# First attention of a two-layer kernel: where the turned row maxima are written, and when

## The reference

```python
qkv = x @ w_in.T + b_in                      # x: 16 batches, turned to 512 positions x 128 channels
q, k, v = jnp.split(qkv, 3, axis=-1)         # 8 heads of 16 channels each
scores = jnp.einsum('bqhd,bkhd->bhqk', q, k) / jnp.sqrt(jnp.asarray(d, q.dtype))
band = jnp.abs(idx[:, None] - idx[None, :]) <= local_size          # 64
scores = jnp.where(band[None, None], scores, neg)
attn = jax.nn.softmax(scores, axis=-1)
o = jnp.einsum('bhqk,bkhd->bqhd', attn, v).reshape(n, t, e)
o = o @ w_out.T + b_out
o = jnp.transpose(o, (0, 2, 1))
y = jax.nn.relu(o) * encodings
out = jnp.einsum('nit,io->not', y, w_ct) + b_ct[None, :, None]
```

## Time and profile before

| | |
|---|---|
| median of the runs | 1466.54 us |
| span of the profiled execution (the page gives no other time of it) | 1463.7 us |
| busy over the span | PE 1354.5 us (93%), DVE 1002.8 us (69%), ACT 791.5 us (54%), POOL 249.2 us (17%) |
| first attention | about the first 490 us of the span |
| its stationary stretch, 130 to 434 us | PE 289.27 us, DVE 290.92 us, ACT 251.25 us of 304 us, full TensorE clock |
| maxima turned (L511) | 32 times, 36.2 to 459.9 us |

### The profile page before, as it was taken

One profiled execution on the slowest core, in us unless ns is written; L12 is line 12 of the kernel. 1 busy time (PEld: TensorE's weight loads), 2 busy tenths in 40 slices (PEclk: granted clock), 3 DMA queues, 4 the chain that ended last, 5 costly groups with the idle time before them and its releaser, 6 DMA issues. The chain is left out here.

```text
span 1463.7 us, 28639 instructions
## 1 busy us (share of the span) xinstructions
PE 1354.5 (93%) x8666; PEld 813.1 (56%) x8666; DVE 1002.8 (69%) x3234; ACT 791.5 (54%) x1802; POOL 249.2 (17%) x265
## 2 busy tenths in 40 slices
PE   3678999999999799999989999999789999999998
PEld 1345555555555444444455555555434777777774
DVE  8889999999997646456546788887659654545211
ACT  4777888888888733332357677776530233332331
POOL 4100000000000100000010000002411255555552
PEclk7699999999999999999999999999999999999999
DMA  8534344343440300000020000000322588888885
GB/s 261 145 87 99 91 107 106 86 119 90 107 104 17 145 1 0 0 0 0 0 75 15 16 16 14 14 1 2 146 85 93 184 247 251 255 257 246 255 233 115
DMA packets 63186, 149.52 MB, mean 102 GB/s; under 512 B 10792, under 2 KB 27830, under 8 KB 58892
## 3 DMA queue, kind: packets, MB, share of 16 engines
q1 hardware_dynamic: 49836, 115.70, 26.1%
q0 software_dynamic: 13280, 32.93, 9.6%
HBM read 113.21 MB, written 35.39 MB: 102 GB/s over the span
## 5 line engine op out<-in xcount | busy, mean ns | idle before, releaser
L776 DVE CUSTOM_DVE_ANT_0 masked_scores<-ps_max,band_mask 128x192 bf16<-128x192 f32 (+1 forms) x512 | 177.2, 383 | 20.5 <-PE ps_max L505 13.9
L383 ACT ACTIVATE probs_t<-ps_sc 128x448 f32<-128x448 f32 x256 | 138.7, 542 | 80.4 <-PE ps_sc L525 78.1
L1255 PE MATMUL f_ps<-f_xt,w_t 128*128 (+1 forms) x704 | 160.2, 382 | 2.5 <-ACT w_t L1310 2.5
L377 ACT ACTIVATE nf_above<-nf_scaled,nf_sign_at 128x512 f16<-128x512 bf16 x231 | 161.5, 715 | 0.0
L2803 DVE TENSOR_TENSOR d_inter<-d_silu_g,d_su 128x384 f32<-128x384 f32 x32 | 17.7, 554 | 159.6 <-PE d_su L2487 154.4
L1927 ACT ACTIVATE c_probs<-d_sg,c_negmax 128x128 f32<-128x128 f32 x256 | 90.3, 365 | 58.1 <-DVE c_negmax L2012 57.7
L1255 PEld LDWEIGHTS f_ps<-f_xt,w_t 128*128 128x128 bf16 x704 | 69.3, 98 | 86.7 <-issue 5.0
L2320 POOL DMA_INDIRECT out<-d_h,d_scatter_now x64 | 97.2, 1519 | 108.3 <-DMA out<-d_h,d_scatter_now 92.9
L505 PE MATMUL ps_max<-k_stack,q_stack 96*128 96x192 bf16 (+1 forms) x512 | 96.5, 272 | 19.8 <-DVE row_max L776 13.8
L2671 DVE TENSOR_SCALAR d_onehot<-d_slot_no,d_pos 128x192 bf16<-128x192 bf16 x512 | 101.0, 288 | 0.3 <-PE d_lb L2388 0.3
L505 PEld LDWEIGHTS ps_max<-k_stack,q_stack 96*128 96x128 bf16 x512 | 46.2, 101 | 92.1 <-issue 46.9
(11 more groups left out here) (381 smaller groups left out, 2830.1 us busy)
## 6 DMA issues: line engine op xcount, KB each, us to landing
d_wgu<-in_ex_gu SPq DMA_DIRECT2D x32, 1024.0 KB
d_wdown<-in_ex_d SPq DMA_DIRECT2D x32, 512.0 KB
dr_parts<-qk_parts SPq DMA_DIRECT2D x32, 384.0 KB, 4.8
q_stack<-dr_parts SPq DMA_DIRECT2D x32, 192.0 KB, 2.7
k_stack<-dr_parts SPq DMA_DIRECT2D x32, 192.0 KB, 3.3
out<-x_sb SPq DMA_DIRECT2D x21, 256.0 KB, 2.2
nf_w<-in_nf_w POOLq DMA_DIRECT2D x3, 1408.0 KB, 10.2
q_stack<-dr_parts SPq DMA_DIRECT2D x32, 128.0 KB, 2.4
```

Of the source, the lines that this page charges most:

```text
L377: act.activation(above[:, g, k, :], lvl[:, g, :], ACT.Sign, bias=cut[:, k - NDV:k - NDV + 1]).then_inc(s_sg, 1)
L383: act.activation(pt[:, c, :], SP[c % 2][:].rearrange("p a w -> p (a w)")[:, a:z], ACT.Exp, scale=D0 ** -0.5).then_inc(s_e, 1)
L776: op = dve.tensor_tensor_reduce(masked[:, c % 2, k, off:off + hi - lo], M[c % 2][:, k, off:off + hi - lo], mask[:, k, off:off + hi - lo], ...
L1255: mm = pe.matmul(bank[:], w12[:, m, kt, ft * P:(ft + 1) * P], xt[:, q, kt, bass.ds(g * N, N)], start=(kt == 0 and q == 0), stop=(kt == KT ...
```

## The change

The turned maxima are written to the unused columns of the edge tile's bank, as two pieces of 64 columns, and three chunks after the half's start instead of at its first or second chunk. The first turn of all, which comes before the batches, stays where it was (`FIRST_MT`).

```diff
+    FIRST_MT, MT, MT_AT = G[0][0:16, 0:P], M[1][0:16, :, WIN - BAND:WIN], QT - 1
...
-            def max_t(u, g):
+            def max_t(u, g, out):
                 pe.wait_ge(s_mx, 8 * u + 8)
-                pe.transpose(G[g][0:16, 0:P], mx[:, g, :], ident[:]).then_inc(s_mT, 1)
+                pe.transpose(out, mx[:, g, :], ident[:]).then_inc(s_mT, 1)
...
# PE, first half
+                    if c == MT_AT:
+                        if not final:
+                            pe.wait_ge(s_mx, 8 * (2 * i + 2) + c - 1)
+                        max_t(2 * i + 1, 1, MT)
                     if not final:
+                        if c == MT_AT + 2:
+                            pe.wait_ge(s_mp, 4 * i + 4)
                         smax(2 * i + 2, 1 - b, 0, c)
...
-                    if c == 0:
-                        pe.wait_ge(s_mp, 4 * i + 2)
-                        ge(pe, s_x1, i - 1)
-                        max_t(2 * i + 1, 1)
...
                     if c == 2 and not last:
-                        pe.wait_ge(s_mp, 4 * i + 4)
+                        ge(pe, s_x1, i - 1)
                         proj(i + 2, b, 1)
...
# PE, second half
                     if not final:
+                        if c == MT_AT:
+                            pe.wait_ge(s_mx, 8 * (2 * i + 3) + c - 1)
+                            max_t(2 * i + 2, 0, MT)
+                        if c == MT_AT + 2:
+                            pe.wait_ge(s_mp, 4 * i + 6)
                         smax(2 * i + 3, 1 - b, 1, c)
...
-                            pe.wait_ge(s_mp, 4 * i + 4)
-                        if not final:
-                            if first:
-                                pe.wait_ge(s_v, 2)
-                            else:
-                                pe.wait_ge(s_on, 2 * i)
-                            if isinstance(i, int) and i == 1:
-                                nf4_mean(1, 3)
-                            max_t(2 * i + 2, 0)
+                            pe.wait_ge(s_x1, i - 1)
+                        if isinstance(i, int) and i == 1:
+                            pe.wait_ge(s_on, 2 * i)
+                            nf4_mean(1, 3)
                         pv(2 * i, b, 0, 1)
...
                     if c == 3 and not first:
-                        if not final:
-                            pe.wait_ge(s_mp, 4 * i + 6)
...
# DVE: the two operations of max_parts, same sizes, now read and written as 16 x 2 x 64
-                dve.tensor_scalar(mparts[:, 0, :], mt, -1.0, None, ALU.mult).then_inc(s_mp, 1)
+                dve.tensor_scalar(turned(mparts[:, 0, :]), mt, -1.0, None, ALU.mult).then_inc(s_mp, 1)
...
# DVE, first half
-                    if c == 1:
-                        max_parts(2 * i + 1, 1)
+                    if c == MT_AT:
+                        max_parts(2 * i + 1, MT)
# DVE, second half
                         take_max(2 * i + 3, 1, c)
-                    if c == 2 and not final:
-                        max_parts(2 * i + 2, 0)
+                        if c == MT_AT:
+                            max_parts(2 * i + 2, MT)
```

More of the change, by code:

```diff
@@ L600, in _ @@
                 if g == 0:
-                    max_t(0, 0)
+                    max_t(0, 0, FIRST_MT)
             pe.wait_ge(s_mp, 2)
@@ L778, in take_max, with max_parts @@
                 op.then_inc(s_mx, 1)
-            def max_parts(u, g):
-                mt = G[g][0:16, 0:P]
+            def max_parts(u, mt):
+                turned = lambda t: t.rearrange("p (a w) -> p a w", w=BAND)
                 dve.wait_ge(s_mT, u + 1)
@@ L787, in max_parts @@
                     ge(dve, s_mw, 16 * (u - 1))
-                dve.tensor_scalar(mparts[:, 0, :], mt, -1.0, None, ALU.mult).then_inc(s_mp, 1)
+                dve.tensor_scalar(turned(mparts[:, 0, :]), mt, -1.0, None, ALU.mult).then_inc(s_mp, 1)
                 dve.wait_ge(s_mp, 2 * u + 1)
-                dve.scalar_tensor_tensor(out=mparts[:, 1, :], in0=mt, scalar=-1.0, in1=mparts[:, 0, :],
+                dve.scalar_tensor_tensor(out=turned(mparts[:, 1, :]), in0=mt, scalar=-1.0, in1=turned(mparts[:, 0, :]),
                                          op0=ALU.mult, op1=ALU.subtract).then_inc(s_mp, 1)
@@ L886, in _ @@
                 take_max(0, 0, c)
-            max_parts(0, 0)
+            max_parts(0, FIRST_MT.rearrange("p (a w) -> p a w", w=BAND))
             for c in range(8):
```

## The result

The changed kernel takes 1473.79 us, the median of four runs (1471.56 to 1475.44). The kernel before takes 1466.32 on the same chip (1461.64 to 1466.81). The ratio is 1.0064, with 95% between 1.0047 and 1.008: slower by 7.5 us, where 1470.5 was forecast, so 4 us. The time lies just above 1473.5, the upper end both of the range that was given and of the forecast's own.

A forecast was written before the change was run, and what follows sets the result against it. Late stack loads were to bound each batch of the first attention: 5.9 + 0.15 + 3.47 + 0.56 + 16.43 = 26.51 us against 26.18, twelve times 0.33 = 4.0 us, giving 1470.5 us; own range 1468.3 to 1473.5, with rivals 1463.0 to 1473.5.

The forecast's parts named there:

- The mechanism: First attention: both PE waits at the turn go, but late stack loads make PE wait and set the period; chance 0.62.
- 0.33 us a batch more: First attention's batches: period 26.51 us against 26.18, over twelve batches behind late loads, 4.0 us in all.
- parts ready to PE's first product (landing and release): From DVE's second-half maxima parts through the last stack load's landing, 5.9 us, to PE's first product, 0.15 more.
- first to third product: PE's first to third maximum product of a batch, without holes: 3.47 us.
- third product to DVE: From PE's third maximum product to DVE's maximum of it: 0.56 us.
- from there to the parts' end: On DVE, from that maximum to the second half's parts: 15.91 us plus 0.52 for the first half's pair, so 16.43.
- The ends together at nothing: Gains and losses outside the stationary batches put at nothing together, between -1.0 and +0.5 us.
- DVE's wait at chunk 2 about 0.85: A sign in the profile: DVE's wait at chunk 2 grows from 0.35 and 0.67 us to about 0.85.
- Rival A: The holes at the turn go and nothing takes their place: 25.9 us a batch, 1463.0 us; chance 0.15.
- Rival B: The loads come late but cost about what the holes did: period 26.0 to 26.25, 1466.5 us; chance 0.15.
- Rival C: PE's projection of V also waits for DVE's chunk 3 residual: 0.3 us a batch on top, 1474 us; chance 0.08.

The follow-up runs named there:

- the loads issued first: The changed kernel with SP issuing the six loads of the next stacks before it waits for the second half's maxima parts: 1461.10 us, ratio 0.9985.
- the added write: The changed kernel with one small unused write to DRAM put in front of the six stack loads on SP: 1480.25 us, ratio 1.0106.
- the control: The kernel before, with SP's six loads moved ahead of the second half's parts and nothing else changed: 1465.27 us, ratio 1.0011.
- the repeated run: The changed kernel timed and profiled once more without any edit: 1473.74 us, ratio 1.0059 against the kernel before.
- the residual ahead of the pair: The changed kernel, six loads issued first, with DVE doing chunk 3's residual before the first half's maxima parts: 1464.41 us, ratio 0.9998.
- The two kernels with the scales earlier: Second batch's block scales one chunk earlier: in the changed kernel, 1474.72 us; with only its second-half change and loads first, 1459.28 us.
- the kernel before with late loads: The kernel before with three small unused writes in front of the six stack loads, delaying them by 1.4 us: 1465.15 us, ratio 1.0004.

## Why the prediction was right, and where it was wrong

**The mechanism: right, and shown.** The two holes at the turn went, the six loads slipped behind SP's write, and PE waits for k_stack 12 times. That these waits decide is shown by the loads issued first (all of the loss gone), by the added write (0.46 us in, 0.5 us a batch out), and by the control, in which the same exchange does nothing. The direction follows from it.

**The size: wrong.** The step that failed is "0.33 us a batch more", 12 x 0.33 = 4.0: the term from the parts to PE's first product was 0.12 us too small, and the 26.18 that the sum was held against 0.05 too large. By terms, for the batch shown above and where there are more, for their mean:

| term | predicted | measured after |
|---|---|---|
| parts ready to PE's first product (landing and release) | 5.87 (taken as 5.9) + 0.15 | 5.86 here; mean of eleven 6.17, in the repeated run 6.31 |
| first to third product | 3.47 | 259.46 - 255.97 = 3.49 |
| third product to DVE | 0.56 | 260.02 - 259.46 = 0.56 |
| from there to the parts' end | 16.43 | 276.40 - 260.02 = 16.38 |
| period | 26.51 | 26.29 for this batch, the shortest of the ten; in the mean 26.63, in the repeated run 26.73 |
| what it is compared with | 26.18 | 26.13 |

Three terms, which were worked out by moving instructions about on paper, held within 0.05 us, and their sum, 20.46, is what the mean batch leaves: 26.63 - 6.17 = 20.46. Two numbers did not hold. The way from the parts to the last landing was read from one batch of the trace before (5.87). The twelve batches of that trace have 5.7 to 6.2, in the mean 6.0, and those of the changed kernel behind the first 5.7 to 6.3, in the mean 6.0: the loads didn't change, I took a batch on the low side. And the baseline of 26.18 was a mean over 12 periods with the longer third batch (26.64) in it, while the sum described a stationary batch, which takes 26.13. Together they turn 0.33 into 0.50 (26.63 - 26.13); the repeated run has 0.60. From the third L810 to the fifteenth, the twelve batches of the forecast, it is 6.0 and 7.2 us in place of 4.0. Of the 3.3 us by which the forecast fell short that is 2.0 to 3.2. The rest, up to 1.3 us, is less than what runs of one kernel differ by, and its cause stays open.

**"The ends together at nothing": too low, not settled.** The rest of the span was to keep its time. It is 1.1 us longer (975.5 for 974.3), in the repeated run 0.8 us. But the profiles of the other ten kernels, whose code behind the last L810 is the same, have 972.7 to 975.8 there, so this is within the differences between executions. The third batch of the profiled execution is 3 us longer. What can be read there is this, on DVE:

```profile
122.10 0.69 DVE L918 SCALAR_TENSOR_TENSOR nf_w<-ps_nf,block_scale 128x512 f32 x1 [1.12 <-DMA block_scale<-dr_rep]
```

then on PE, and in the windows of the changed kernel and of its repeated run:

```profile
122.94 1.01 PE L573 MATMUL ps_nf<-nf_above,ident_f 128*128 128x512 f16 x2 [2.35 <-DVE nf_w L918]
```
```profile
102.00:106.00 4.00, 3.79 (x26) 2.30 (x27) 2.60 (x13) 1.25 (x3) 0.00 (x0) 0.57 0.83 180
122.00:126.00 4.00, 3.06 (x7) 1.39 (x8) 2.19 (x9) 0.01 (x1) 0.00 (x0) 0.59 0.06 14
```
```profile
122.00:126.00 4.00, 4.00 (x22) 2.23 (x21) 3.34 (x18) 1.98 (x4) 0.00 (x0) 1.00 0.00 0
```

The granted clock, the number before the last two, is 0.57 and 0.59 in two stretches of the one and 1.00 in the later of them in the other. In the first of them DVE runs late, the scales are sent late, L918 waits for them, PE stands 2.35 us, and the clock is at its lower level again. The same pair of events is in one more kernel (the residual ahead of the pair, with a third batch of 30.12), and in none of the others. That the slow stretch at 102 us begins it is argued from the order in time. The two kernels with the scales earlier have the slow stretch, not the wait, and no long third batch; the wait alone, 1.06 us at full clock, is in the kernel before with late loads, with a third batch of 27.78. This fits the account and doesn't settle it, and moving the scales earlier did not lower the median.

**What would show it.** Waits for x_sb and o_rows gone: right. 11 or 12 waits for k_stack of 0.5 to 0.9 us: 12, 10.8 us in all, but of 0.5 to 1.4, five of them above 0.9. SP's write of the parts 1.5 us nearer to the batch's end: the parts end 5.48 us before L810 starts where they ended 7.25 before it, 1.8 nearer. L810 each 26.5: 26.63. DVE's wait at chunk 2 about 0.85: 0.64, with 0.17 at chunk 3, where the turn's cost was put. The stretch 16.4: 16.38.

**Rival A** was priced right and given for the wrong kernel: 25.9 us a batch when the loads don't bind is what the loads-first kernel shows (25.86), and its gain of 3.5 us is near the 3.9 that kernel has. Its condition, a landing within 5.3 us of the parts, was missed by 0.7. **Rival B** needed 0.3 us less in the landing; it went the other way. **Rival C** saw the right wait (12 times 0.6 us for the residual; it had some 0.5) and the wrong price: in the kernel with the loads first its removal gives nothing back, and in the changed kernel the stretch on DVE in which it lies took 16.38 us, no more than the 16.43 reckoned without it. It was not removed in the changed kernel itself. Its time, 1474, is the measured one by chance.

The Trainium skill has a figure for the largest term, in "DMA: Bandwidth & Descriptors", "Anatomy of one DMA — SWDGE (gpsimd) path": a fixed cost of about 2.0 us plus the bytes at 436 GB/s, an estimate of 2.3 us for the last load of 128 KB. It is given for DMAs that gpsimd issues, and SP issues these. The trace shows another time for them: the 144 stack loads of the changed kernel land after 2.1 to 3.5 us, in the median 3.0, as before. With 2.3 in the sum in place of some 3.1 the period would have come out at 25.7, and the change as a gain.

## What to carry to other kernels

Before an operation is moved later, look at which in-order queue waits for its result and what stands in it behind: the slack of those transfers is in no list of waits, and must be reckoned from landing to first use. A short wait that is removed may have been the cover of another one; close holes one at a time, and exchange queue entries so that what is ready goes first. In a sum for a ring of dependencies take each term as the mean over all batches, and compare it with the stationary period, not with a mean that holds the first batches.

## What the runs showed of the hardware

**An issue on a queue can cost a batch its full time.** One write of 16 x 128 elements, 0.35 us on SP's queue and 0.46 by which the loads began later, made each batch 0.5 us longer behind the parts, with six loads queued behind it. The Trainium skill says in "DMA: Bandwidth & Descriptors", "Issuing engines are not separate DMA queues", that the time to initiate a DMA is usually small relative to the DMA itself. The trace agrees for one (0.42 us of issue to 3.0 of landing), but the six in a row take 2.6 us (276.93 to 279.56), nearly as much as the landing.

**A strided access costs nothing here.** The maxima read and written as 2 x 64 columns take what the 128 in a row took (a median of 274 ns for L788 and 279 for L790, in both kernels):

```profile
L788 DVE TENSOR_SCALAR max_parts<-ps_max x24: 273/274/275, 128.8 to 435.6; 16x128 bf16<-16x128 f32 x24
```

**The scatter between runs.** Runs of one kernel lie within 4 to 11 us of each other. In the profiles read in steps of half a us, TensorE's granted clock falls to its lower level, 1.2 GHz, for mostly 3.4 us at a time, at places that differ from run to run: in eleven of the thirteen profiles it does so between 111 and 120 us, and in the other two, the ones with the long third batch, at 102 or 104 and again at 123 or 125 us. In four (the kernel before, the changed kernel twice, and that with later loads) it falls once more, between 445 and 465 us, and the batch then takes 26.6 to 27.2 us for 24.2 to 25.1 in the nine others. Some 2 us of the scatter are thus seen; what makes it fall there in one execution and not in the next stays open. A profile of one execution can't tell differences of a few us: without the repeated run, 3 of the 10 us would have been put down to the change.
